# Delta attention on one core: compact ACT and DVE operands in the block inverse, one addition moved from DVE to POOL, and a new order on PE, ACT, DVE and POOL

## The reference, cut to what matters

```
q, k, v = silu(conv4(x @ Wq.T)), silu(conv4(x @ Wk.T)), silu(conv4(x @ Wv.T))
v_hat = k @ Wsv.T ; e = v_hat - v
s = [sqrt(sum e*e + eps), sum |e|, 1 - cos(v_hat, v)]      # three statistics of a token
beta, amp = sigmoid(mlp_b(s)), mlp_a(s)
g = -exp(A_log) * softplus(amp * k / |k| + dt_bias)        # decay of each channel
for t:  S = S * exp(g_t);  delta = (v_t - k_t S) * beta_t;  S = S + k_t delta;  o_t = q_t S
o = rmsnorm(o) * norm_w * sigmoid(x @ Wg1.T @ Wg2.T + bg2);  out = o @ Wo.T
```

## Time and profile before

| | |
|---|---|
| Median of three runs | 7889.38 us (7876.38 to 7897.79) |
| The profiled execution's own time | 7873.47 us |
| Its span, first to last instruction | 7871.7 us |
| Mean granted TensorE clock (1 is 2.4 GHz) | 0.863 |
| PE busy | 6441.0 us (82%) |
| DVE busy | 5383.5 us (68%) |
| ACT busy | 4036.5 us (51%) |
| POOL busy | 2781.6 us (35%) |
| DMA | 172.75 MB, mean 22 GB/s |

### The profile page before, as it was taken

One profiled execution on the slowest core, in us unless ns is written; L12 is line 12 of the kernel. 1 busy time (PEld: TensorE's weight loads), 2 busy tenths in 40 slices (PEclk: granted clock), 3 DMA queues, 4 the chain that ended last, 5 costly groups with the idle time before them and its releaser, 6 DMA issues. The chain is left out here.

```text
span 7871.7 us, 201064 instructions
## 1 busy us (share of the span) xinstructions
PE 6441.0 (82%) x70112; PEld 4584.8 (58%) x70113; DVE 5383.5 (68%) x11406; ACT 4036.5 (51%) x7866; POOL 2781.6 (35%) x4659
## 2 busy tenths in 40 slices
PE   6879999878278888888888888888888888799483
PEld 5768999644145555555555555555555555588342
DVE  6966666542367777777788787778777777544464
ACT  2323333112156666766676666666666666355021
POOL 2300000121245545555555555455545555100403
PEclk9988888789588889988899998889888888788597
DMA  0000000112100000000000000000000000000223
GB/s 30 0 17 4 5 4 4 45 55 87 48 12 14 12 14 12 14 12 14 12 14 12 14 14 12 12 14 14 12 12 14 12 14 10 11 9 8 101 63 93
DMA packets 136085, 172.75 MB, mean 22 GB/s; under 512 B 29104, under 2 KB 110096, under 8 KB 135184
## 3 DMA queue, kind: packets, MB, share of 16 engines
q1 hardware_dynamic: 122896, 135.34, 5.7%
q0 software_dynamic: 13056, 35.67, 1.4%
HBM read 128.74 MB, written 42.21 MB: 22 GB/s over the span
## 5 line engine op out<-in xcount | busy, mean ns | idle before, releaser
L2830 PEld LDWEIGHTS d_ps_tx<-d_W,d_NT 64*64 64x64 f32 x10240 | 379.5, 143 | 393.6 <-issue 393.5
L2412 DVE TENSOR_TENSOR d_kq<-d_qkv,d_pre 128x512 f32<-128x512 f32 x768 | 530.4, 691 | 96.1 <-issue 92.8
L2372 DVE SCALAR_TENSOR_TENSOR d_y<-d_ps_kv,d_head,d_y 128x504 f32<-128x504 f32 (+2 forms) x768 | 554.4, 722 | 60.9 <-ACT d_y L2593 42.0
L2752 PE MATMUL d_ps_kv<-d_xnT,d_wqkv 128*128 (+1 forms) x1024 | 581.9, 696 | 4.2 <-DVE d_y L2372 3.2
L1502 POOL MEMSET m_earlier<- 128x64 f32 x2 | 0.3, 152 | 1568.4 <-POOLq L2987 1568.4
L2290 POOL TENSOR_TENSOR d_lnu<-d_lnu,d_z 128x512 f32<-128x512 f32 x128 | 162.9, 1273 | 1007.0 <-ACT d_lnu L2634 1007.0
L2830 PE MATMUL d_ps_tx<-d_W,d_NT 64*64 64x64 f32 x10240 | 467.4, 234 | 46.3 <-DVE d_W L2458 36.6
L2458 DVE TENSOR_TENSOR d_W<-d_W,d_ps_tx 128x256 f32<-128x256 f32 x512 | 213.9, 418 | 425.2 <-PE d_ps_tx L2842 425.2
L2817 PEld LDWEIGHTS d_ps_level<-d_kq,d_ks 128*64 128x64 f32 x10240 | 411.6, 162 | 148.5 <-DVE d_kq L2412 101.8
L2817 PE MATMUL d_ps_level<-d_kq,d_ks 128*64 128x64 f32 x10240 | 487.0, 253 | 3.3 <-DVE d_kq L2412 3.3
L2256 POOL TENSOR_TENSOR d_roots<-d_radicand,d_power 128x20 f32<-128x20 f32 x128 | 460.0, 3593 | 10.1
(11 more groups left out here) (460 smaller groups left out, 17629.0 us busy)
## 6 DMA issues: line engine op xcount, KB each, us to landing
d_wqkv<-in_d_wqkv SPq DMA_DIRECT2D x128, 384.0 KB, 3.1
m_xg<-m_rows_in SPq DMA_DIRECT2D x144, 128.0 KB, 2.0
m_rows_out<-m_ye SPq DMA_DIRECT2D x144, 128.0 KB, 1.7
b_ctx<-in_ctx SPq DMA_DIRECT2D x64, 128.0 KB, 2.0
d_wg<-in_d_wg SPq DMA_DIRECT2D x128, 64.0 KB, 2.6
x_sb<-in_x SPq DMA_DIRECT2D x8, 512.0 KB, 7.5
m_wgu<-in_m_wgu SPq DMA_DIRECT2D x2, 2048.0 KB
out<-x_sb SPq DMA_DIRECT2D x8, 512.0 KB, 5.7
```

What stands on the lines that cost most here:

```text
L2372: ins = nc.vector.scalar_tensor_tensor(out3, in3, head[A.i][:, tap:tap + 1], out3, ALU.mult, ALU.add)
L2412: nc.vector.tensor_tensor(dst, src, by, ALU.mult).then_inc(sems["kq_ready"], 1)
L2752: last = nc.tensor.matmul(ps_qkv[j], wqkv[u.i][:, j, kt, :], xnT[:, kt, tokens(u)], start=(kt == 0), stop=(kt == KT - 1))
L2830: last = nc.tensor.matmul(ps_t[rows, j * S:(j + 1) * S], NT[rows, l - 1, j, :], W[i][rows, 0, j, :], start=True, stop=True)
```

## The change

Four things. First, `product_t` reads W with the columns of each level in another order, the lower half block first (`lower_first`), so that the 32 columns of T that matter stand in columns 0 to 31; all 64 still move through PE. `copy_t` copies only these 32 of each 64, `T` is zeroed once at the start, and `next_w` subtracts only 32 columns of each 64 (the left half blocks of W; at the last level the right half of the transposed W). Second, `softplus_sum` goes from DVE to POOL, behind `add_positive`. Third, all four lists have a new order, and the step boundaries lie elsewhere: `value_guess`, `sums`, `silu`, `squares` and `own_product` of a unit are now done when it is B, the first product of the inverse when it is D, and `deltas`, `outputs` and the last `copy_t` when it is E. Fourth, `lower` moves out to where all engines' code sees it.

```diff
+        def lower_first(ap, s):
+            return ap.rearrange("p (n two s) -> p two n s", two=2, s=s)
...
+                def softplus_sum(B):
+                    pool.wait_ge(sems["pos_added"], B.n)
+                    hold(sems["soft_ready"], nth(B, 3, 2))
+                    nc.gpsimd.tensor_tensor(lnu, lnu, rest, ALU.add).then_inc(sems["soft_ready"], 1)
...
+                first(nc.vector.memset(T[:, :, :], 0.0))
...
-                def softplus_sum(B):
-                    dve.wait_ge(sems["soft_ready"], nth(B, 3, 2))
-                    dve.wait_ge(sems["pos_added"], B.n)
-                    nc.vector.tensor_tensor(lnu, lnu, rest, ALU.add).then_inc(sems["soft_ready"], 1)
...
-                    less = ps_x.rearrange("p (j n) -> p j n", j=4)
+                    less = ps_x.rearrange("p (j n) -> p j n", j=4)[:, :, 0:HALF] if l < LEVELS - 1 else ps_x.rearrange("p (j n) -> p j n", j=4)[:, :, HALF:S]
                     if l < LEVELS - 1:
-                        nc.vector.tensor_tensor(W[i][:, 0, :, :], W[i][:, 0, :, :], less, ALU.subtract).then_inc(sems["w_sub"], 1)
+                        s = 2 ** l
+                        left = W[i][:, 0, :, :].rearrange("p j (n two s) -> p j n two s", two=2, s=s)[:, :, :, 0, :]
+                        nc.vector.tensor_tensor(left, left, less.rearrange("p j (n s) -> p j n s", s=s), ALU.subtract).then_inc(sems["w_sub"], 1)
...
-                        nc.vector.tensor_tensor(W[i][:, 1, :, :], W[i][:, 1, :, :], less, ALU.subtract).then_inc(sems["w_step"], 1)
+                        nc.vector.tensor_tensor(W[i][:, 1, :, HALF:S], W[i][:, 1, :, HALF:S], less, ALU.subtract).then_inc(sems["w_step"], 1)
...
-                    nc.scalar.copy(T[:, :, :], ps_t.rearrange("p (j n) -> p j n", j=4)).then_inc(sems["t_ready"], 1)
+                    nc.scalar.copy(T[:, :, 0:HALF], ps_t.rearrange("p (j n) -> p j n", j=4)[:, :, 0:HALF]).then_inc(sems["t_ready"], 1)
...
-                        last = nc.tensor.matmul(ps_t[rows, j * S:(j + 1) * S], NT[rows, l - 1, j, :], W[i][rows, 0, j, :], start=True, stop=True)
+                        last = nc.tensor.matmul(ps_t[rows, j * S:(j + 1) * S], NT[rows, l - 1, j, :], lower_first(W[i][rows, 0, j, :], 2 ** l), start=True, stop=True)
```

More of the change, by code:

```diff
@@ L2482, in vector_step @@
                 def vector_step(A, B, C, D, E):
+                    if D:
+                        masked(D, 5)
+                    if B:
+                        errors(B)
                     if A:
@@ L2485, in vector_step @@
                     if D:
-                        next_w(D, 3)
+                        next_w(D, 1)
+                    if E:
+                        mean_squares(E)
+                    if C:
+                        level_keys(C, 0)
+                        level_keys(C, 1)
+                        level_keys(C, 2)
+                        level_keys(C, 3)
+                    if E:
+                        gated(E)
+                    if D:
+                        next_w(D, 2)
+                    if C:
+                        level_keys(C, 4)
+                        masked(C, 0)
+                        masked(C, 1)
+                    if D:
+                        next_w(D, 3)
+                    if C:
+                        level_keys(C, 5)
+                    if A:
+                        taps(A, VALUE, 2)
+                    if D:
+                        next_w(D, 4)
+                    if E and E.i == 1:
+                        added(E, 0)
+                    if A:
+                        taps(A, QUERY, 3)
                     if B:
@@ L2669, in scalar_step @@
                 def scalar_step(A, B, C, D, E):
+                    if E:
+                        copy_t(E, 5)
+                    if B:
+                        silu(B, KEY, 1)
+                        silu(B, VALUE, 2)
+                        silu(B, QUERY, 3)
+                    if C:
+                        decay_sizes(C)
+                    if A:
+                        first_tap(A, KEY, 1)
+                    if C:
+                        decay_logs(C)
+                    if E:
+                        deltas_out(E)
+                    if D:
+                        copy_t(D, 1)
                     if B:
@@ L2888, in tensor_step @@
                 def tensor_step(A, B, C, D, E):
+                    if A:
+                        projection(A, KEY, 1)
+                    if B:
+                        value_guess(B)
+                    if E:
+                        deltas(E)
+                        gate_product(E)
+                    if D:
+                        product_t(D, 1)
+                    if C:
+                        turn_values(C)
+                    if E:
+                        outputs(E)
+                    if D:
+                        product_x(D, 1)
+                    if A:
+                        projection(A, VALUE, 2)
+                        projection(A, QUERY, 3)
+                    if B:
+                        sums(B)
+                    if C:
+                        level_product(C, 0)
+                    if B:
+                        turn_sums(B)
+                    if E:
+                        turn_outputs(E)
                     if D:
@@ L2931, in tensor_step @@
                     if D:
-                        deltas(D)
-                    if A:
-                        value_guess(A)
+                        product_t(D, 3)
+                        product_x(D, 3)
+                    if C:
+                        level_product(C, 3)
+                    if D:
+                        product_t(D, 4)
+                    if B:
+                        turn_features(B)
+                    if C:
+                        level_product(C, 4)
+                    if B:
+                        hidden_layer(B)
+                    if D:
+                        product_x(D, 4)
+                    if C:
+                        level_product(C, 5)
+                    if B:
+                        second_layer(B)
+                    if D:
+                        product_t(D, 5)
+                    if B:
+                        spread(B)
                     if E and E.i == 1:
@@ L2937, in tensor_step @@
                     if D:
[L2938 to L2952 removed]
+                        product_x(D, 5)
                 run_units(pe, tensor_step)
```

166 lines of the change are left out of this document (36 added, 130 removed).

## The result

The changed kernel takes 7435.43 us (median of four, 7434.0 to 7436.66) against 7889.4: a ratio of 0.9426, with a 95% interval of 0.941 to 0.9442.

What follows compares the result with a forecast made beforehand. A ring of waits between engines bounds the delta attention; its full-clock unit falls from 33.3 to 32.0 us, clock loss stays 2.6. 1.3 x 128 = 166 us less gives 7707, shown as 7723 us; range 7570 to 7860.

Steps and rivals of the forecast that it cites:

- The ring: Delta attention's loop of waits between engines, from one unit's `sums` to the next: 33.31 us falls to 31.95 at full clock.
- (d): Ring piece from `decay_scale` on POOL through spread, decay input and exponential to the logarithm's end: 7.61 to 7.8 us.
- (a): Ring piece from the start of `sums` on PE to the first feature instruction on POOL: 4.07 to 4.1 us.
- (c): Ring piece from the features' turn through the two layers on PE and ACT to `decay_scale`: 4.15 to 4.6 us.
- (e): Ring piece from the logarithm's end through ACT's list to the next `sums`: 9.13 to 7.1 us, without silus and guess.
- For the clock I add the same 2.6 us as today: Term for TensorE's lower clock in the mean unit, kept unchanged: 32.0 becomes 34.6 us, against 35.9 before.
- Rival 1: Clock recovers as the 3 us pause before `deltas` goes: half of 2.6 us a unit returns, 7556 us; chance 0.16.
- Rival 3: PE's packed stretch after the features' turn meets the low clock: unit 36.2 us, 7927 us in all; chance 0.16.
- Rival 2: A table load at the loop's head delays the absolute value 1.2 us in every other unit: 7800 us; chance 0.12.
- Rival 4: POOL's addition and `own_product` hold DVE's level keys through the shared port, up to 1.3 us a unit: 7889; chance 0.06.
- Strided reads on PE: Products' moving operand read with a stride: between nothing and 0.6 us for each of five products; taken as nothing.
- The edits: Compact copies save 0.5 us of ACT and 0.7 of DVE a unit; the softplus addition moves 1.6 us off DVE.

Runs made afterwards that it cites:

- fill_new: The changed kernel plus four useless matmuls on PE in units without an output projection, their output overwritten by `gate_product`: 7287.35 us, ratio 0.9221.
- old_pool_sum: The kernel before with only the last softplus addition moved from DVE to POOL, behind `add_positive`: 7919.77 us, ratio 1.0037.

## Why the prediction was wrong

- **The ring** was the right bound and its pieces were nearly right: 31.95 forecast, 31.62 measured with the output projection. (d) was 0.8 too short there, as DVE's taps come late in that unit in full and ACT waits 0.4 us for the key projection; (a), (c) and (e) were 0.5, 0.4 and 0.3 too long. The other unit is shorter by 0.84 us (30.78, shown by `fill_new`), where 31.95 was a mean over two kinds that I had only 0.4 apart. With 31.20 as the mean, the ring gave 2.10 us a unit, 267 of 431 us, where I had 1.35, or 172.
- **The step that failed** is "For the clock I add the same 2.6 us as today". It measured 32.50 - 31.20 = 1.3 us, so 1.3 less than the sum has. This is 1.3 x 127, some 164 us, and the larger part of the 259 that were missing; the ring's 95 are the rest. Rival 1 had the size of this term (half of the loss comes back), at 0.16, and its 7556 lacked the ring's 95. Its reason, that the pause before `deltas` goes, is not what the runs show: a filler in that pause, in every other unit, gave the old kernel 0.3%, so that its size came true is luck. Why half of the loss came back stays open. I argued against the rival with a pause of 3 us before the features are turned; it was 0.7 to 1.0, since PE does `product_t(D, 4)` only from 10.1 to 10.8 us after `sums` (the row at 4289.08 above), with the output projection from 10.6 to 11.3, and rival 1 has it stand from about 9 on. From a term of 2.6 us of which I could say neither its cause nor its course in the new order, I should have given both directions equal weight, and let the range reach it.
- **The clock's mechanism** was right in part: filling the pause before the features recovers 3% in the old kernel, and filling the pauses of every other unit 2% in the new. Filling my other pause, before `deltas`, takes slow stretches away (56 to 21) and hardly any time. And pauses of the same length stand in units with and without a slow stretch.
- **Rival 3**, slow PE in the packed stretch: the slow stretch does reach into it, but in the unit with slack. 10.24 us at 1.2 GHz cost 2.45 us there, and none fell into the full unit. A product took 1.12 us in it against 0.68, so PE did more than the half that I had reckoned with.
- **Rival 2** did not occur: four groups of table loads remain, 128 or 127 each, none at the head of the loop. ACT went from 24.1 to 22.0 us a unit. DVE's 25.6 was too low: it stands at 26.8 on average (27.75 and 25.89), for 27.9 was the lower of the old kernel's two kinds and the addition's mean there is 1.41 us, not the median of 1.64.
- **Rival 4, the lock**: the level keys are not held, their 128x512 instruction takes 684 ns at the median and 696 at most between 2500 and 6200 us. They run so even beside POOL's power instruction of 3.59 us (L2262), which reads SBUF too. POOL's moved addition takes 1275 ns, as priced, and `own_product` fell from 1765 to 1270 as it no longer meets a two-operand DVE instruction. One new meeting was missed. In the timeline of the unit with the projection, POOL's `scaled_masks` holds the first instruction of `softplus_rest` until 4334.1:

```profile
4332.84 1.25 POOL L2229 TENSOR_TENSOR d_mask_a<-d_masks,d_small 128x640 f32<-128x640 f32 x1 [0.92 <-DVE d_NT L2449]
...
4333.35 1.02 DVE L2400 TENSOR_SCALAR d_sumsT<-d_u 128x512 f32<-128x512 f32 x1 [0.39 <-ACT d_u L2634]
```

  It took 0.42 us before. The Trainium skill (SBUF — State Buffer, on which operations take the shared pair) names `tensor_scalar` among the DVE operations that can contend with POOL, and this row agrees. The delay does not reach the next `sums` in this unit: PE waits 0.43 us for DVE's `added` behind it and still has 0.38 over before `sums`.
- **Strided reads on PE** cost nothing: a product is 0.68 us in both kernels. **The edits** I had as almost free of effect on the path. Singly they nearly are (- 21 and + 32 us when undone); together they carry 87 us (102 in medians), which was not in the sum, because I had placed the new lists with the shorter DVE work already in them and never asked what the lists would do without.

## What to carry to other kernels

When engines wait for each other in turn, follow one ring of waits through all of them; it gave the mean full-clock unit to 2.4% here (31.95 against 31.20). Then treat TensorE's clock as a term of its own, read from units at either level: it was 2.6 of 35.9 us, it moves with any reordering, and it can eat a gain (`old_pool_sum`) or double one. Where PE pauses shortly and the clock drops behind it, a piece of useless work in the pause is a cheap test, and here also the fastest kernel of the study (7287 us). Moving fewer columns in as many matmul instructions, which hardly shortened them here (0.66 us against 0.68), can cost more than it gives.

## What the runs showed of the hardware

- One useless 128x512 product of 1.0 us a unit made the old kernel 3% faster, and four 128x256 ones in every other unit the new one 2%.
- Sixteen 64x64 matmul instructions take 0.68 us with 64 moving columns and 0.66 with 32, at the same clock; with 32 the mean granted clock of the run fell from 0.877 to 0.836.
- The slow stretches of the changed kernel are locked to its pair of units: 10.24 us in each pair of 64.85 us, 11.4 to 12.5 us after `sums`. The old kernel's wandered (13 to 37 us after `sums`), and its units took 33.3 to 37.6 us.
- DVE's two-operand instructions from SBUF took 0.68 us beside POOL's power instruction of 3.59 us, as by themselves; POOL's 128x512 product took 1.77 us where it met one of DVE's and 1.27 where it did not.
- What stays open: why the clock falls in one place and not in another. Work in a pause and the columns moved both change it in these runs, units with pauses of the same length go either way, and by what rule is not settled; nor was it tried whether a smaller filler would do.
